# A state-space layer and a two-expert mixture on one core: unsplit fp32 products in attention, routing one chunk sooner, second-layer weights copied by an SP transfer

## What is computed

```
# "attention": a linear recurrence with 32 complex states, then a two-layer network
Bu = x @ Bn.T ;  s_t = lam * s_(t-1) + Bu_t           # over the 256 rows of a sequence
y  = Re(s @ C.T) + x @ D.T
z  = gelu_tanh(y @ W1) @ W2                           # 128 -> 512 -> 128
x1 = layernorm(x + x + sigmoid(res) * z)
# "ffn": each row goes to the 2 of 8 experts with the highest softmax(x1 @ Wg)
out_e = gelu(x1 @ W1[e] + b1[e]) @ W2[e] + b2[e]      # 128 -> 512 -> 128
out   = layernorm(x1 + sum over both experts of weight * out_e)
```

## Time and profile before

| | us |
|---|---|
| median of 3 runs | 371.14 (370.22 to 372.06) |
| span of the profiled execution | 385.0 |
| its own time beside the span | not given; the span alone is above all three runs |
| busy: PE / DVE / ACT / POOL | 275.6 / 278.8 / 233.1 / 226.1 |
| granted TensorE clock, mean | 0.878 |

### The profile page before, as it was taken

How to read it: one execution, slowest core, us unless ns; L and a number is a source line. 1 busy time by engine, 2 the same in 40 slices (tenths; PEclk the granted TensorE clock), 3 DMA queues, 4 the chain that set the end, 5 groups by cost and what they waited for, 6 DMA issues and landing times.

```text
span 385.0 us, 5368 instructions
## 1 busy us (share of the span) xinstructions
PE 275.6 (72%) x1329; PEld 225.6 (59%) x1329; DVE 278.8 (72%) x791; ACT 233.1 (61%) x498; POOL 226.1 (59%) x281
## 2 busy tenths in 40 slices
PE   1467998699867739339643039999999999962940
PEld 1234776377535429239533029999999999941410
DVE  2999889999984978409931027999999999930680
ACT  2406665577753756508731037999999999950461
POOL 4888156638867767710677724666666766671460
PEclk9999999789979968958986558999999999995885
DMA  3633203101101122120222213222222222115732
GB/s 103 197 95 115 78 1 109 56 0 49 43 28 48 43 69 64 42 56 22 58 88 99 95 63 104 84 83 86 82 85 81 68 84 83 61 43 207 282 103 82
DMA packets 27189, 31.19 MB, mean 81 GB/s; under 512 B 4632, under 2 KB 22560, under 8 KB 27160
## 3 DMA queue, kind: packets, MB, share of 16 engines
q1 hardware_dynamic: 22328, 20.89, 18.0%
q0 software_dynamic: 4832, 9.97, 7.7%
HBM read 16.99 MB, written 13.86 MB: 80 GB/s over the span
## 4 chain that ended last, share of the span: by engine, by line
DVE 41%; issue 20%; PE 15%; POOL 9%; DMA 5%; ACT 4%; DVEq 1%; another core or an unknown queue 1%; SPq 1%; ACTq 0%; POOLq 0%
DVE h_l L928 8%; DVE wuse L891 7%; POOL slots_d L448 5%; DVE h_h L924 4%; PE bank L1028 3%; PE bank L1030 3%; PE bank L1029 3%; DVE work L693 2%; DVE h_l L697 2%; POOL results_d L454 2%; PE bank L1170 2%; PE bank L1178 1%; ACT fw L616 1%; DVE xt_l L914 1%; DMA late<-slots_d 1%
## 5 line engine op out<-in xcount | busy, mean ns | idle before, releaser
L454 POOL DMA_INDIRECT results_d<-work,dest x87 | 88.7, 1019 | 54.6 <-ACT work L590 34.1
L448 POOL DMA_INDIRECT slots_d<-rows,slot_i x64 | 66.6, 1040 | 38.6 <-DVE rows L830 19.4
L574 ACT ACTIVATE h<-bank,buse 128x384 f32<-128x384 f32 x116 | 67.8, 584 | 32.8 <-issue 21.5
L928 DVE TENSOR_TENSOR h_l<-h,h_h 128x384 fp32r<-128x384 f32 x116 | 64.5, 556 | 27.4 <-ACT h_h L579 23.6
L1028 PE MATMUL bank<-h_h,wuse 128*128 128x384 f32 (+1 forms) x148 | 60.5, 409 | 3.9 <-DVE h_l L697 1.6
L1028 PE MATMUL bank<-xt_h,wuse 128*128 128x384 f32 x116 | 42.2, 364 | 26.1 <-issue 20.2
L1029 PE MATMUL bank<-h_l,wuse 128*128 128x384 f32 (+1 forms) x148 | 53.3, 360 | 0.0
L1030 PE MATMUL bank<-h_h,wuse 128*128 128x384 f32 (+1 forms) x148 | 53.2, 360 | 0.0
L520 ACT ACTIVATE h<-bank 128x512 f32<-128x512 f32 x32 | 19.0, 595 | 38.3 <-DVE h_l L697 18.8
L891 DVE CAST wuse<-fw 128x1024 fp32r x58 | 40.0, 691 | 1.4 <-issue 1.4
L1029 PE MATMUL bank<-xt_l,wuse 128*128 128x384 f32 x116 | 40.8, 352 | 0.0
(11 more groups left out here) (213 smaller groups left out, 610.4 us busy)
## 6 DMA issues: line engine op xcount, KB each, us to landing
late<-slots_d SPq DMA_DIRECT2D x29, 195.0 KB
late<-in_L_ffn_W_dram SPq DMA_DIRECT2D x16, 256.0 KB, 2.8
work<-in_L_attn_x3d_dram SPq DMA_DIRECT2D x8, 256.0 KB, 3.3
rows<-results_d SPq DMA_DIRECT2D x4, 512.0 KB, 5.1
work<-results_d SPq DMA_DIRECT2D x4, 512.0 KB, 8.5
out_dram<-fw SPq DMA_DIRECT2D x8, 256.0 KB, 2.3
slots_d<-zeros SPq DMA_DIRECT2D x9, 195.0 KB, 4.1
results_d<-work,dest POOLq DMA_INDIRECT x87
```

The source lines that it names most:

```text
L448: pool.indirect_dma_start(out=slots_d, out_offset=bass.IndirectOffsetOnAxis(ap=slot_i[:, k, i:i + 1], axis=0), in_=rows[:, k, i, :], in_of ...
L454: pool.indirect_dma_start(out=results_d, out_offset=bass.IndirectOffsetOnAxis(ap=dest[:, SQ * g + q:SQ * g + q + 1], axis=0), in_=yo[:, g ...
L574: act.activation(h32[:, b % 2, 0:SLOTS], H_PS[b % 2][:, 0:SLOTS], ACT.Gelu, bias=buse[:, k, b:b + 1]).then_inc(sm["gelu_b"], 1)
L928: dve.tensor_tensor(ht_l[b], h32[:, b % 2, 0:SLOTS], ht_h[b].bitcast(F32), ALU.subtract).then_inc(sm["hbl_ready"], 1)
```

## The change

- Attention's B, D and second-layer products take plain fp32 operands: one matmul in place of three, no high and low parts of x and of the hidden layer. The first layer keeps its triple.
- Groups 0, 1 and 2 are routed in chunks 2, 4 and 6 (`routed_in`), their weights at the head of the next chunk, tiles planned in chunks 5 and 7. Statistics, rows and the back transpose of chunk c-1 come earlier in chunk c. The last group is routed at cuts 1, 2 and 4 of `walk`, its exponential on ACT at cut 3.
- `weights2` copies only the bias; SP copies a tile's second-layer weights from `fw` to `wuse` in SBUF (`second_weights`), and PE waits for that transfer.
- Expert weights are loaded at once, straight into `fw`, and split in place by POOL without pauses except three norms; SP writes two zero tails at each of the tiles 4 to 7 instead of all eight ahead of tile 9; four places for x instead of two.
- Setup: some transfers are issued by ACT, its copies of the transposed matrices and of W1 replace DVE's; two small norm operations go from POOL to DVE; PE transposes tile 0 inside chunk 7, ahead of its second layer.

```diff
-        ROUTING = {GC * g + GC + 1: g for g in range(NG - 1)}
+        def routed_in(c):
+            return (c - 2) // GC if c >= 2 and c % GC == 0 else None
...
+            def second_weights(g):
+                e = sp.value_load(experts[0:1, g:g + 1], min_val=0, max_val=E - 1)
+                wait(sp, sm["zb_ready"], HB * (g - 1))
+                sp.dma_start(wuse[g % 2][:, 2:4, :].rearrange("p a h -> p (a h)").bitcast(F32),
+                             fw[:, bass.ds(e, 1), 2 * H:4 * H].rearrange("p a h -> p (a h)").bitcast(F32)).then_inc(w2_loaded[g % 2], 16)
             for n in range(PHASES):
+                if n:
+                    second_weights(begins[n] - 1)
                 if n == PHASES - 1:
-                    zero_tails()
                     sp.wait_ge(sm["prefilled"], 16)
                     sp.wait_ge(sm["tails_zero"], 16 * E)
                 sp.wait_ge(sm["route_ready"], n + 1)
                 sp.wait_ge(dispatched[n + 1], 16 * 2 * GT)
                 for g in range(begins[n], ends[n]):
                     load(g, g % 2)
+                    if g == 1:
+                        sp.wait_ge(sm["fw_lo"], NFW)
+                        second_weights(0)
+                    if g == 2:
+                        sp.wait_ge(sm["pre_a"], HB * NCH)
+                    if g >= 2 and g not in begins:
+                        second_weights(g - 1)
+                    if TAILS <= g < TAILS + E // 2:
+                        if g == TAILS:
+                            sp.wait_ge(sm["tails_ready"], 1)
+                        zero_tails(2 * (g - TAILS))
+                        zero_tails(2 * (g - TAILS) + 1)
...
# POOL
-            for c in range(NCH + 2):
-                if c >= 2:
-                    norm(c - 2)
-                for n in pieces(c):
-                    weights(n)
-                if c >= GC + 2:
-                    dispatch((c - GC - 2) // GC, (c - GC - 2) % GC)
+            for e in range(E):
+                for a in range(2):
+                    weights(e, a)
+                if e in (4, 6, 7):
+                    norm((4, 6, 7).index(e))
+            for g in range(NG - 1):
+                dispatch(g, 0)
+                if GC * g + 3 < NCH:
+                    norm(GC * g + 3)
+                dispatch(g, 1)
+                if GC * g + 4 < NCH:
+                    norm(GC * g + 4)
...
# DVE
+            def chunk(c):
+                g = routed_in(c)
+                if c + 1 < NCH:
+                    turn_back(c + 1, 0)
+                    turn_back(c + 1, 1)
+                if c >= 1:
+                    if g is None and c >= 3:
+                        route_weights(routed_in(c - 1))
+                    stats(c - 1)
+                    aggregate(c - 1)
+                    logits(c - 1)
+                if g is not None:
+                    route_choice(g, 0)
+                    route_choice(g, 1)
+                    route_hits(g)
+                if c + 1 < NCH:
+                    y_low(c + 1)
+                if g is not None:
+                    route_exponents(g)
+                elif c >= 5:
+                    route_tiles((c - 5) // GC)
+                if c + 2 < NCH:
+                    turn_in(c + 2)
+                if c == NCH - 1:
+                    first_tile()
+                residual(c)
+                if g is not None:
+                    route_ranks(g)
+                    route_slots(g)
...
-            walk(dve, MT, step, {ROUTE3: last_stats, ROUTE3 + 1: last_ranks,
-                                 ROUTE3 + 2: lambda: route_slots(NG - 1), ROUTE3 + 3: last_weights})
+            walk(dve, MT, step, {1: last_choice, 2: last_slots, 4: last_weights})
...
# PE
             def inputs(c):
-                products(BU_PS[:], bt_h[:], bt_l[:], xt_h[:, c % 2, :], xt_l[:, c % 2, :], True, True).then_inc(sm["bu_ready"], 1)
+                mm(BU_PS[:], bt, xt32[:, c % 3, :], start=True, stop=True).then_inc(sm["bu_ready"], 1)
...
                 if c + 1 < NCH:
                     outputs(c + 1)
+                if c == NCH - 1:
+                    xt(0, 0)
                 for b in range(HB):
-                    pe.wait_ge(sm["hl_ready"], HB * c + b + 1)
-                    products(Z_PS[:], w2_h[:, b * D:(b + 1) * D], w2_l[:, b * D:(b + 1) * D], h_h[:, b, :], h_l[:, b, :],
-                             b == 0, b == HB - 1).then_inc(sm["z_ready"], 1)
+                    pe.wait_ge(sm["h_act"], HB * c + b + 1)
+                    mm(Z_PS[:], w2[:, b * D:(b + 1) * D], h32[:, b, :], start=b == 0, stop=b == HB - 1).then_inc(sm["z_ready"], 1)
...
                 if now:
-                    pe.wait_ge(sm["w2use_ready"], g + 1)
+                    pe.wait_ge(w2_loaded[k], 16 * (g // 2 + 1))
```

More of the change, by code:

```diff
@@ L141, in build @@
         cre, cim = early[:, 4 * P:4 * P + NS], early[:, 4 * P + NS:4 * P + 2 * NS]
-        bt_h, bt_l = sb("bt_h", [P, P], F32R), sb("bt_l", [P, P], F32R)
-        dt_h, dt_l = sb("dt_h", [P, P], F32R), sb("dt_l", [P, P], F32R)
-        wcs = sb("wcs", [P, 2, P])
+        turned = sb("turned", [P, 4, P])
+        bt, dt, wcs = turned[:, 0, :], turned[:, 1, :], turned[:, 2:4, :]
         wuse = [sb(f"wuse{i}", [P, 4, H], F32R) for i in range(2)]
-        w1_h, w1_l, w2_h, w2_l = (wuse[1][:, n, :] for n in range(4))
+        w1_h, w1_l = (wuse[1][:, n, :] for n in range(2))
         wg = sb("wg", [P, E])
         wgc = sb("wgc", [P, E])
-        fst = late[:, 2 * CHUNK:4 * CHUNK].rearrange("p (a h) -> p a h", a=2)
         fw = sb("fw", [P, E, 4 * H], F32R)
@@ L304, in _, with weights @@
-            sp.dma_start(bst[:, 0:H], fb1).then_inc(sm["bias_loaded"], 16)
-            sp.dma_start(bst[:, H:H + D], fb2).then_inc(sm["bias_loaded"], 16)
-            def weights(n):
-                wait(sp, sm["fw_lo"], n - 1)
-                sp.dma_start(fw_stage_in(n), fw_src(n)).then_inc(fst_loaded[n % 2], 16)
-            for n in range(2):
-                weights(n)
+            def weights(e):
+                sp.dma_start(fw_part(e, 0, 1).bitcast(F32), FW1[e]).then_inc(fw_loaded[e], 16)
+                sp.dma_start(fw_part(e, 1, 1).bitcast(F32).rearrange("p (c d) -> p c d", c=HB),
+                             FW2[e].rearrange("(c p) d -> p c d", p=P)).then_inc(fw_loaded[e], 16)
@@ L315, in zero_rows @@
+            weights(0)
+            sp.dma_start(xr[:, 2], x_t[2]).then_inc(xr_loaded[2], 16)
+            weights(1)
+            sp.dma_start(xr[:, 3], x_t[3]).then_inc(xr_loaded[3], 16)
+            for e in range(2, E):
+                weights(e)
             def zero_rows(row):
@@ L490, in x_copy @@
                 wait(act, sm["r_ready"], c - 2)
[L491 to L493 removed]
+                act.copy(xt32[:, c % 3, :], XT_PS[:]).then_inc(sm["xt_sb"], 1)
             def rows_of(c):
@@ L545, in _ @@
             x_copy(0)
+            act.wait_ge(sm["setup_t"], 1)
+            act.copy(turned[:, :, :].rearrange("p a n -> p (a n)"), Z_PS[:]).then_inc(sm["setup_sb"], 1)
             act.wait_ge(sm["tables_ready"], 1)
@@ L1059, in outputs @@
                 mm(Y_PS[:], wcs[:, 1, :], qs, start=False, stop=False)
-                products(Y_PS[:], dt_h[:], dt_l[:], xt_h[:, c % 2, :], xt_l[:, c % 2, :], False, True).then_inc(sm["y_ready"], 1)
+                mm(Y_PS[:], dt, xt32[:, c % 3, :], start=False, stop=True).then_inc(sm["y_ready"], 1)
             def chunk(c):
```

291 lines of the change are left out of this document (110 added, 181 removed).

## The result

| | before | after |
|---|---|---|
| median, us | 370.95 (369.23 to 372.06, 5 runs) | 341.08 (340.64 to 342.72, 5 runs) |
| ratio | | 0.9195, interval 0.9155 to 0.9236 |
| span of the profiled execution | 385.0 | 340.7, its own time 342.72 |
| spans of the other runs after | | 338.6 to 339.4 beside times of 340.64 to 341.15 |

The account below looks back on a forecast made before the run. The path was taken as GpSimd's dispatch queue up to tile 9, then TensorE's expert loop: tile 9 at 186 + 102.3 + 43.1 = 331.4 against 362, -30.6; from median 371.1 that gives 340.5, called 341, range 323 to 363.

Parts of the forecast that it names:

- 362 against 371.1: 9 us lie around it: Kernel before: undisturbed span 362, with tile 9 at about 217, against the runs' median 371.1; 9 us lie outside the span.
- GpSimd's price: Send-backs at the end: 87 at 1.26 us each from 181.5, 109.6 us in all, ending at 291.
- not the bound, with 4 us to spare: GpSimd's send-backs end at 291, while the last tile's rows are sent by 295 anyway, so they do not bound.
- worth nothing in the loop: Expert loop: taking 29 weight copies of 0.69 us off VectorE gains 0 to 0.1 us a tile, TensorE being full.
- the copy was the bound: Rival, chance 0.08: VectorE's weight copy bounds the expert loop; tiles would fall to 4.2 us, GpSimd capping the time near 335.
- The difference, -30.6: Whole kernel: span 331.4 after the change against 362 undisturbed before, taken off the median 371.1 to give 340.5.
- covered by the fifth half: Dispatch: GpSimd wants norm(7) at 128, hidden behind the fifth half; if not, each us of it moves the end.
- the chunk starts: Attention: chunks 0 to 3 start at 23.5, 36.5, 48 and 61 us, plain ones 11.4 apart.
- rival two: Chance 0.20: VectorE is late in routing chunks beside GpSimd's weight splits; first dispatch at about 78, +10 us, time 351.
- the zero tails' long run a stray: Before tile 9: SP's eight zero-tail transfers of 28.49 us make a hole in the profiled execution, explaining its long span.
- no slower side: Slower had chance 0.05: the SBUF weight transfer over 5.5 us would delay tiles, 371 at 8.5 us and 381 at 9.5.
- The 3.5 taken for the transfer: Expert loop: SP's SBUF copy of second-layer weights lands after 3.5 us, hidden within 6.1 us available.

Follow-up runs that it names:

- experiment 1: The changed kernel with the second-layer weights copied by VectorE again and no transfer inside SBUF: 353.94 us, ratio 0.9576.
- experiment 2: The changed kernel with all eight zero-tail transfers issued together again, ahead of tile 9's load: 347.96 us, ratio 0.9423.
- experiment 3: The kernel before with only the zero tails spread two by two behind the loads of tiles 4 to 7: 371.69 us, ratio 1.0045.
- Experiment 7: The changed kernel with tile 0's transposes behind chunk 7's second layer and chunk 7's statistics ahead of them: 339.10 us, ratio 0.9178.
- experiment 4: The kernel before with only the second-layer weights copied by SP's transfer inside SBUF: 367.52 us, ratio 0.9916.
- experiment 6: The changed kernel with the first-layer weights of tiles 2 to 28 also copied by an SP transfer inside SBUF: 340.36 us, ratio 0.9192.
- experiment 10: The changed kernel with four more 128x512 SBUF-to-SBUF subtractions on VectorE at the head of each attention chunk: 355.25 us, ratio 0.9517.
- experiment 5: The kernel before with both the second-layer weights by SP's SBUF transfer and the zero tails spread over tiles 4 to 7: 360.43 us, ratio 0.9646.
- experiment 9: The changed kernel routing its first three groups in chunks 3, 5 and 7, with tile 0's transposes behind chunk 7: 347.22 us, ratio 0.9301.

## Why the prediction was right, and where it was not

*Around the span (wrong).* "362 against 371.1: 9 us lie around it" failed. 2 us do. The undisturbed kernel before spans 364.5 to 369.8 in its runs beside experiments 1, 2, 3 and 7, up to 373.3 on another chip. The missing 6 us or so were inside: tile 9 comes at about 221, not 217 (experiment 4), and the send-backs are a second bound (experiment 3). These are the nearest traces; none of the kernel before itself without the hole was kept. I should have asked why a span and a time differ by so much, not have taken the difference as given.

*GpSimd's price and "not the bound, with 4 us to spare" (wrong).* The term "87x1.26 = 109.6, end 291" measured 117.7 to the end at 304.6: 5.5 us from a later start, 8.1 from the pace of 1.36. 1.26 was (88.7+20.5)/87 of the earlier trace rows. But a send-back that waited for rows has its gap of 0.30 booked under that wait, and so the 20.5 us lack some 19 such gaps: 1.019+0.30 = 1.32 was in the same row and gives 114.8, most of the miss. 1.26 is a floor (0.96+0.30), and not the price under VectorE's load.

*The transfer "worth nothing in the loop" (wrong).* For TensorE it is, as said: tiles 4.85 and 4.86 us apart. But it is worth 12.9 us in the changed kernel (experiment 1), by way of GpSimd: a copy on VectorE holds up a send-back, and so does a subtraction of two SBUF operands (experiment 6). The rival "the copy was the bound" had named the right cap (GpSimd) and the wrong path to it. I weighed the Trainium skill's port rule for attention alone, beside GpSimd's weight splits, and not in the expert loop, where it decides.

*These errors cancel, and that is luck.* The level of before was put 6 to 7 us too low and that of after, 331.4, about 8 too low (median span 339.2). The difference, -30.6, measured -29.9. How the profiled 340.7 stands to 331.4, by how late each step was: first dispatch 2.2 (69.7 against 67.5), end of the fourth half 0.6 (116.1 against 115.5, the halves were quicker than priced), of the sixth 3.0 (143.3 against 140.3, norm(7)), tile 3 3.7, the last group 5.6 (165.6 against 160), tile 9 6.7 (192.7 against 186), end of the last product 7.5 (295.8 against 288.3); behind it 44.9 us instead of 43.1, GpSimd's lag, make 9.3. The profiled run is itself 1.5 above the median.

*Norm(7) "covered by the fifth half" (wrong).* It was 3.2 us late, because tile 0's rows came at 121.15, chunk 7's residual at 128.15. Experiment 7 takes it away.

*Right.* An fp32 product of 512 columns 0.86 us (two records of L1056, 0.43 apart); the chunk starts 24.3, 36.4, 47.8 and 60.4 (23.5, 36.5, 48 and 61 forecast), though of the plain chunks only chunk 1 took 11.4, chunks 3 and 5 12.3 and 12.5 with TensorE idle 0.6 and 0.8 us; VectorE late far less where it routes than before the change (rival two, 0.20, did not come, though experiment 10 shows that four more subtractions a chunk bring it, at 355); the transfer at 3.2; tiles at 4.86; the zero tails' long run a stray; no slower side. The 3.5 taken for the transfer was a guess between bounds, since no row had its time.

*Where the 30 us come from.* The ratios make a chain. Transfer and tails in the kernel before: 3.5%, 13 us (experiment 5; 10 by the medians). From there to the changed kernel routed later with tile 0 behind (experiment 9, on the same chip): another 3.5%, 13 us; that is the setup, the unsplit products and whatever else the change holds. Sooner routing: 1.2%, 5 us (experiments 7 and 9; 8 by the medians). Tile 0's early place takes back 0.2%, 0.6 us (2 by the medians, 4 in the traces). No run parts the setup from the unsplit products. The traces say this much: chunk 0 starts at 24.3 instead of 28.0, and chunk 3, in which experiment 9 and the kernel before both route, takes 11.9 us instead of 19.9. That the unsplit products' relief of VectorE does this is argued from experiment 10, and not shown by taking them back.

## What to carry to other kernels

A queue that looks idle part of the time is priced by its saturated pace under the other engines' load, not by its mean duration; ask for the queue's end again after every gain upstream. Two bounds a few us apart make each single edit look worthless: try them together. A wait put in front of the work that feeds the queue it waits for costs little when early and all of it when late.

## What the runs showed of the hardware

A GpSimd indirect DMA issue took 0.96 us, 1.26 apart, beside an idle VectorE. In the expert loop they came 1.33 us apart on the mean (waits left out) with no 128x1024 fp32 copy per tile on VectorE, 1.36 with one, 1.41 and 1.47 with two; single ones went to 1.70. One that met a VectorE copy, or a subtraction with both operands in SBUF, near its start ended 0.82 to 0.85 us behind that operation; one that met a copy near its end, 0.11 to 0.13 behind it. Beside ten subtractions with one operand in PSUM none was stretched. A transfer of 512 KB inside SBUF, issued by SP, landed after 3.2 us and slowed no tile. Eight zero transfers of 195 KB took SP 8.6 and 8.7 us to issue while the dispatches landed, 28.5 in one stray execution. An fp32 product of 512 columns took 0.86 us. Two VectorE subtractions of 128x512 with operands in SBUF took 2.4 to 2.8 us while GpSimd split weights, 1.3 without. In the first chunk that routes, TensorE, idle 30% of the time, was granted 0.83 of its clock on the mean, between its levels of 1.2 and 2.4 GHz, where after the change it was granted all of it.
